# Cross-attention and routed FFN on one core: a ring of eight gathered units, x2 in its own column order, w1 loaded through a permuted view

## The chip, the core and the metric

The kernel runs on one core of a Trainium2 chip. The metric is device time in microseconds, start to end of one execution. The kernel before was run three times unprofiled: 381.10, 386.09 and 389.21 us, median 386.09 us.

## What is computed

The input x is 8 batches of 100 tokens with 512 columns; ctx is 8 batches of 722 rows of 512 columns. Everything is fp32.

```python
def _L0_xattn_ref(x, w1, v1, w2):          # w1 = v1 = w2 = ctx
    x1 = jnp.einsum('eth,efh->etf', x, w1)
    x2 = jnp.einsum('eth,efh->etf', x, v1)
    h = jax.nn.gelu(x1, approximate=True) * x2
    return jnp.einsum('etf,efh->eth', h, w2)
...
def _L0_ffn_ref(h, router_w, w1, b1, w2, b2):
    logits = x @ router_w                   # 16 experts
    assign = jnp.argmax(logits, axis=-1)
    w = jax.nn.sigmoid(jnp.take_along_axis(logits, assign[:, None], axis=1)[:, 0])
    hh = jnp.einsum('nd,edf->nef', x, w1) + b1      # 512 -> 1024
    hh = jax.nn.gelu(hh, approximate=False)
    all_out = jnp.einsum('nef,efd->ned', hh, w2) + b2   # 1024 -> 512
    out = jnp.take_along_axis(all_out, assign[:, None, None], axis=1)[:, 0, :]
    out = out * w[:, None]
...
x = x + _L0_xattn_ref(_layernorm(x, axis=-1), ctx_1024, ctx_1024, ctx_1024)
x = x + _L0_ffn_ref(_layernorm(x, axis=-1), ...)
```

So each of the 800 tokens goes to one of 16 experts, and an expert's weights are 512x1024 (w1) and 1024x512 (w2).

## The kernel before

Work falls into three parts.

**Attention, one batch after another** (NB = 8). TensorE multiplies the layer-normed batch with ctx (`hidden`), ScalarE and VectorE make the gated hidden rows, TensorE multiplies back (`attention`). VectorE adds x (`add_x2`), giving x2, in one of two buffers `xw` of 100 x 4 x 132: four pieces of 128 columns with four more numbers each (a zero, mean, inverse deviation, gate). GpSimd writes a batch's `xw` to the DRAM table `rows` (`put_rows`). Before the change a piece holds columns in a permuted order (`"p (k g r) -> p g k r"`), so that a 32x32 block transpose later gives rows of x in the order in which w1 lies.

**Units.** Tokens are sorted by expert into units of U = 32 tokens. A unit is gathered from `rows` into one slot of the ring `grow` (128 partitions = 4 pieces x 32 tokens) by an indirect DMA of GpSimd (`take`), with indices from the table `lin`. The first four units belong to experts 0 to 3 and are planned from the first six batches alone (`tab_e`, gathered at L887). The table `lin` of all other units (28 here) is made after the last batch: counts on TensorE, `plan_ends`, `token_weights`, `tokens`, `plan_units` on VectorE, `all_slots` on TensorE, `unit_table` on VectorE.

**A unit's work.** VectorE: `fetch` (normalise the gathered rows, and a copy `rb` of them), `turn_tokens` (block transpose to `xT`), `hidden` (transpose and bias, two halves), `residual` and `finish` (scale, add, write to `y`). TensorE: `first_layer` (two halves), `residual` (four matmuls with the identity, which bring x2's rows back to column order), `second_layer`. ScalarE: Gelu. GpSimd, in program order in `step`: copy an index column, wait until the gather of unit i+3 has landed (`landed`), wait for `finish` of its unit, scatter the result to `out` (`put_out`, which then waits for the scatter before it and frees a `y` buffer, of which there are two), and gather unit i+4 (`take`). The order on each engine is the program's order; semaphores tie them. VectorE cannot write `y` (L721) before GpSimd has freed a buffer (`s_yfree`, L838).

**Weights.** SyncE issues every load. There are five slots of w1 and w2 (4 MB of fp32 per expert). Experts 0 to 3 go to `W_early`: one piece (a quarter of an expert, 1 MB) per batch among the ctx loads, eight pieces behind them; expert 4 goes to `area` when ctx has left it. Expert e from 5 on is loaded when expert e-5 has done its last unit: w1 after its first layer (`s_h`), w2 after its second (`s_y`). A piece is one transfer of 128 partitions x 8 KB.

Of the kernel before, what the change touches and what calls it, by code (L numbers as in the profile page):

```python
# [14 lines left out]
P = 128  # L15
# [13 lines left out]
EARLY = 4  # L29
NT = TOK // U - 1  # L30
# [43 lines left out]
def build(nc, x, ctx_main, ctx_rest, ctxT_a, ctxT_b, router, w1, b1, w2, b2, consts, out):  # L74
# [5 lines left out]
    with ExitStack() as stack:  # L80
# [19 lines left out]
        grow = sb("grow", [P, EARLY, ROW])  # L100
        res = sb("res", [P, P])
        unit = sb("unit", [P, 4 * KF * U])
        tb, rb, xT, rT = (sb(n, [P, P]) for n in ("tb", "rb", "xT", "rT"))
        tab_e, lin = sb("tab_e", [P, EARLY], U32), sb("lin", [P, NU], U32)
        idx, at = ([sb(f"{n}{i}", [P, 1], U32) for i in range(2)] for n in ("idx", "at"))
# [5 lines left out]
        zt, gate = sb("zt", [T, 1]), sb("gate", [T, 1])  # L111
# [13 lines left out]
        y = unit[:, 6 * KH * U:8 * KH * U]  # L125
        tok_e = unit[0:T, 0:EB * P].rearrange("p (b q) -> p b q", b=EB)
        tok_all = area[0:T, 2 * WL:2 * WL + NB * P].rearrange("p (b q) -> p b q", b=NB)
# [27 lines left out]
        p_hh, p_r = (p_h[:, 0:P], p_two[:, 0:P]), p_xb[:, 320:320 + P]  # L155
# [5 lines left out]
        s_b2q, s_r = sem("s_b2q"), sem("s_r")  # L161
        s_w = [sems(f"s_w{i}_", 4) for i in range(SLOTS)]
        s_row, s_er = sems("s_row", 2), sems("s_er", EARLY)
        s_g, s_done = sems("s_g", Q), sems("s_done", 2)
# [47 lines left out]
        def _(sp):  # L212
# [21 lines left out]
            def load_w(e, piece):  # L234
                w, src = (W1, w1) if piece < 2 else (W2, w2)
                n = (KD, KF)[piece // 2] // 2
# [14 lines left out]
            for k in range(KD):  # L251
                sp.dma_start(rw[U * k:U * k + U], router.rearrange("(g r) k e -> k r g e", g=Q)[k]).then_inc(s_con, 16)
# [48 lines left out]
        def _(pe):  # L301
# [58 lines left out]
            def all_slots():  # L360
                pe.wait_ge(s_tok, 1)
# [9 lines left out]
            def first_layer(v, e, half):  # L371

                slot, landed = e % SLOTS, 16 * (e // SLOTS) + 16
# [20 lines left out]
            def second_layer(v, e):  # L394

                slot, landed = e % SLOTS, 16 * (e // SLOTS) + 16
                pe.wait_ge(s_yo, v)
                for c in range(KF):
# [7 lines left out]
                last.then_inc(s_y, 1)  # L406
# [3 lines left out]
            for b in range(NB):  # L410
# [5 lines left out]
                hidden(b, 0)  # L416
                if b > 0:
                    transpose_x2(b - 1)
# [5 lines left out]
                else:  # L424
                    pe.wait_ge(s_con, 16 + 16 * KD)
# [8 lines left out]
                if b == FIX + 2:  # L434
                    early_slots()
# [15 lines left out]
            residual(1)  # L451
            logits(NB - 1)
            second_layer(1, 0)
            ranks(NB - 1)
            first_layer(2, 1, 0)
            counts(NB + 1)
            first_layer(2, 1, 1)
            residual(2)
# [3 lines left out]
            residual(3)  # L462
# [3 lines left out]
            residual(4)  # L466
            all_slots()
            second_layer(4, 3)

            def unit_of(e, i):  # L470
                v = pe.snap(i + (EARLY + 1))
                first_layer(v, e, 0)
                first_layer(v, e, 1)
                residual(v)
                second_layer(v, e)
# [5 lines left out]
        def _(act):  # L481
# [21 lines left out]

            copy_rows(xnT, p_t, s_xnps, s_xnT, 0)
# [9 lines left out]

            copy_rows(x2T, p_t, s_x2ps, s_x2T, NB - 1)
# [16 lines left out]
        def _(dve):  # L532
# [137 lines left out]
            def tokens():  # L670
                dve.wait_ge(s_rest, NB)
                nc.vector.tensor_tensor(tok_all, t_row.unsqueeze(1).to_broadcast([T, NB, P]),
                                        rest_all[:, :].unsqueeze(2).to_broadcast([T, NB, P]), ALU.is_equal
                                        ).then_inc(s_tok, 1)

            def unit_table():
                dve.wait_ge(s_linps, 1)
                nc.vector.tensor_scalar(lin[:, :], p_lin, far_col, None, ALU.add).then_inc(s_lin, 1)
# [4 lines left out]
            def row_of(j):  # L683
                at0 = of(j % Q) * ROW
# [23 lines left out]
            def residual(j, v, e):  # L708

                dve.wait_ge(s_r, v)  # L710
                nc.vector.transpose(rT[:, :], rb[:, :])
                nc.vector.scalar_tensor_tensor(out=res[:, :], in0=b2s[:, e, :], scalar=row_of(j)(P + 3, 1), in1=p_r,
                                               op0=ALU.mult, op1=ALU.add).then_inc(s_res, 1)

            def finish(j, v):
# [4 lines left out]
                to = of(j % 2) * P  # L720
# [4 lines left out]
            dve.sem_inc(s_y, 1)  # L725
            nc.vector.memset(p_xb[U * 2:P, 2 * T:3 * T], 0.0).then_inc(s_zero, 1)
            nc.vector.memset(xw[:, :, :, P:P + 1], 0.0)
            nc.vector.memset(first_area[3 * U:P, 0:XR * D + D], 0.0).then_inc(s_zero, 1)
# [6 lines left out]
            dve.wait_ge(s_con, 16 + 16 * KD)  # L735
            for b in range(NB):
# [3 lines left out]
                if b + 1 < NB:  # L740
                    x_stats(b + 1)
                multiply(b, 0)
# [11 lines left out]
                if b == FIX + 2:  # L754
                    early_table()
# [4 lines left out]
            nc.vector.transpose(rT[:, :], rb[:, :]).then_inc(s_res, 1)  # L760
# [8 lines left out]
            residual(0, 1, 0)  # L769
            route(NB - 1)  # L770
            place_rows(NB - 1)
            write_gate(NB - 1)

# [6 lines left out]
            residual(1, 2, 1)  # L780
            plan_ends()
            token_weights()
            tokens()
# [7 lines left out]
            residual(2, 3, 2)  # L791
            plan_units()
# [4 lines left out]
            unit_table()  # L797
# [3 lines left out]
            residual(3, 4, 3)  # L801

            def unit_of(e, i):
# [7 lines left out]
                residual(i + EARLY, v, e)  # L811
# [5 lines left out]
        def _(pool):  # L817
# [13 lines left out]
            def put_out(j, r, index):  # L831

                nc.gpsimd.indirect_dma_start(out_q, bass.IndirectOffsetOnAxis(ap=index, axis=0),  # L833
                                             y[:, P * (r % 2):P * (r % 2) + P], None,
# [5 lines left out]
            def take(i, r):  # L840

                nc.gpsimd.tensor_copy(idx[r % 2][:, :], lin[:, bass.ds(i, 1)]).then_inc(s_idx, 1)  # L842
                pool.wait_ge(s_idx, number(i + 1))
                pool.sem_inc(s_apart_p, 1)  # L844
                nc.gpsimd.indirect_dma_start(grow[:, r, :], None, rows_q,  # L845
                                             bass.IndirectOffsetOnAxis(ap=idx[r % 2][:, :], axis=0),
                                             bounds_check=bound_piece, oob_is_err=False).then_inc(s_g[r], 16)

            def landed(i, r):
                pool.wait_ge(s_g[r], number(4 * i + (16 - 4 * r)))  # L850
                pool.sem_inc(s_rows, 1)  # L851

            def step(i, r):

                nc.gpsimd.tensor_copy(at[r % 2][:, :], lin[:, bass.ds(i, 1)]).then_inc(s_at, 1)  # L855
                landed(i + (Q - 1), (r - 1) % Q)
# [3 lines left out]
                put_out(i + EARLY, r, at[r % 2][:, :])  # L860
                take(i + EARLY, r)

            def early_step(j):
                pool.wait_ge(s_yo, j + 2)
                landed(j - 1, (j - 1) % Q)
# [90 lines left out]
```

## Time and profile before

| | |
|---|---|
| three runs, median | 386.09 us (381.10 to 389.21) |
| the profiled execution | 381.66 us, span 379.6 us, mean granted TensorE clock 0.887 |
| TensorE matmuls busy | 267.8 us, 71% |
| VectorE / ScalarE / GpSimd busy | 137.6 / 39.8 / 103.3 us |
| moved by DMA | 99.46 MB |

The span is the time from the first to the last instruction. The page of the profile cuts it into 40 slices of 9.49 us. "Busy" is instruction time; an engine that waits is not busy. The idle time before an instruction is put down to what released it; GpSimd's "POOLq L838" is its sequencer at line 838. "issue" is waiting that the profile cannot put down to anything. The DMA share is the mean busy share of the core's 16 DMA engines.

### The profile page before, as it was taken

To read this page: it belongs to the slowest core of one execution; us is meant where nothing else is said; L and a number is where in the kernel's file an instruction comes from. 1 tells how busy PE (TensorE), PEld (TensorE's weight loads), DVE (VectorE), ACT (ScalarE), POOL (GpSimd) and SP (SyncE) were. 2 spreads that over 40 slices of the span, in tenths; PEclk is the share of its full clock that TensorE was granted. 3 is DMA by queue.
4 is the path that set the end of the run, shared out by engine and by line. 5 is a ranking of instruction groups with operands and counts; after the bars stand their busy time and mean duration, and the time that the engine had idled before them with its cause. 6 is when DMAs were issued, how large, how long until landed. Compare 5 with 4: busy or idle time off the path is not lost.

```text
span 379.6 us, 12189 instructions
## 1 busy us (share of the span) xinstructions
PE 267.8 (71%) x5032; PEld 228.2 (60%) x5032; DVE 137.6 (36%) x534; ACT 39.8 (10%) x107; POOL 103.3 (27%) x157
## 2 busy tenths in 40 slices
PE   0999989999997956855649456767575667577610
PEld 0868856876693856745548355667474667467510
DVE  3016434644443751532233333222233143525410
ACT  1201111111110200010000000000000001101000
POOL 1002102211114122422234323322232134435451
PEclk9999999999999979896798987688779669989975
DMA  7989999999999992099940999999908940000000
GB/s 267 329 279 299 270 330 342 377 362 347 377 386 412 416 403 82 16 360 416 416 183 11 355 414 418 413 364 377 404 13 321 417 194 16 22 17 23 20 7 6
DMA packets 19704, 99.46 MB, mean 262 GB/s; under 512 B 4072, under 2 KB 4528, under 8 KB 11348
## 3 DMA queue, kind: packets, MB, share of 16 engines
q1 hardware_dynamic: 16852, 93.91, 65.8%
q0 software_dynamic: 2816, 5.03, 4.0%
q8 instruction: 27, 0.44, 0.5%
q14 instruction: 9, 0.07, 0.1%
HBM read 96.33 MB, written 3.82 MB: 264 GB/s over the span
## 4 chain that ended last, share of the span: by engine, by line
DMA 33%; issue 14%; POOL 8%; POOLq 2%
DMA grow<-rows,idx 33%; POOL out L833 6%; POOL idx L842 2%; POOLq L842 0%; POOLq L837 0%; POOL grow L845 0%; POOLq L908 0%; POOLq L858 0%; POOLq L855 0%; POOLq L850 0%; POOLq L844 0%; POOLq L838 0%; POOLq L859 0%; POOLq L851 0%; POOLq L857 0%
## 5 line engine op out<-in xcount | busy, mean ns | idle before, releaser
L403 PE MATMUL bank<-W_early,unit 128*32 128x128 f32 x1600 | 63.9, 326 | 55.6 <-issue 55.5
L403 PEld LDWEIGHTS bank<-W_early,unit 128*32 128x32 f32 x1600 | 56.2, 132 | 61.0 <-issue 60.9
L381 PE MATMUL bank<-W_early,xT 128*32 128x128 f32 x1600 | 58.6, 305 | 11.6 <-DVE xT L696 7.8
L721 DVE SCALAR_TENSOR_TENSOR unit<-bank,grow,res 128x128 f32 (+1 forms) x32 | 11.2, 350 | 140.4 <-POOLq L838 129.5
L381 PEld LDWEIGHTS bank<-W_early,xT 128*32 128x32 f32 x1600 | 52.7, 125 | 15.3 <-DVE xT L696 8.9
L833 POOL DMA_INDIRECT out<-unit,at x28 | 29.1, 1040 | 116.5 <-issue 116.5
L316 PE MATMUL bank<-xnT,area 128*128 128x100 f32 (+1 forms) x384 | 51.7, 290 | 0.6 <-ACT xnT L484 0.6
L316 PEld LDWEIGHTS bank<-xnT,area 128*128 128x128 f32 (+1 forms) x384 | 48.7, 202 | 4.4 <-issue 3.5
L328 PE MATMUL bank<-area,hidT 128*100 128x512 f32 (+1 forms) x96 | 44.7, 604 | 1.8 <-DMA area<-in_ctx_rest 1.6
L501 ACT ACTIVATE unit<-unit 128x128 f32<-128x128 f32 x64 | 19.7, 310 | 215.8 <-DVE unit L703 215.7
L845 POOL DMA_INDIRECT grow<-rows,idx x32 | 35.3, 1102 | 25.6 <-POOL idx L842 24.9
L403 PE MATMUL bank<-area,unit 128*32 128x128 f32 x448 | 18.4, 333 | 15.3 <-issue 15.3
L328 PEld LDWEIGHTS bank<-area,hidT 128*100 128x100 f32 (+1 forms) x96 | 15.2, 171 | 20.3 <-issue 17.7
L403 PEld LDWEIGHTS bank<-area,unit 128*32 128x32 f32 x448 | 16.5, 136 | 16.9 <-issue 16.9
L820 POOL TENSOR_TENSOR xw<-ve_t,con 100x4 f32<-100x4 f32 x8 | 8.5, 1069 | 54.9 <-DVE ve_t L564 54.9
L701 DVE STREAM_TRANSPOSE unit<-bank 128x128 f32<-128x128 f32 x64 | 19.8, 310 | 1.6 <-PE bank L381 1.5
L703 DVE TENSOR_TENSOR unit<-unit,b1s 128x128 f32<-128x128 f32 x64 | 18.9, 295 | 2.2
L553 DVE TENSOR_TENSOR xw<-first_area,bank 100x512 f32<-100x512 f32 x8 | 5.5, 683 | 33.5 <-PE bank L328 33.5
L691 DVE TENSOR_SCALAR tb<-grow 128x128 f32 (+1 forms) x33 | 12.3, 372 | 13.1 <-DMA grow<-rows,tab_e 6.9
L381 PE MATMUL bank<-area,xT 128*32 128x128 f32 x448 | 14.7, 285 | 0.7 <-issue 0.7
L381 PEld LDWEIGHTS bank<-area,xT 128*32 128x32 f32 x448 | 13.5, 117 | 1.2 <-issue 1.1
L390 PE MATMUL bank<-con,rT 128*32 128x128 f32 x256 | 13.6, 277 | 0.0
(89 smaller groups left out, 201.1 us busy)
## 6 DMA issues: line engine op xcount, KB each, us to landing
W_early<-in_w SPq DMA_DIRECT2D x52, 1024.0 KB, 11.8
area<-in_w SPq DMA_DIRECT2D x12, 1024.0 KB, 10.9
area<-in_ctxT_a SPq DMA_DIRECT2D x8, 768.0 KB, 10.6
area<-in_ctx_main SPq DMA_DIRECT2D x8, 768.0 KB
area<-in_ctxT_b SPq DMA_DIRECT2D x8, 676.0 KB, 11.0
area<-in_ctx_main SPq DMA_DIRECT2D x8, 512.0 KB
rows<-xw POOLq DMA_DIRECT2D x8, 206.2 KB, 7.3
first_area<-in_x SPq DMA_DIRECT2D x8, 192.0 KB
```

The source lines that it names most:

```text
L316: last = nc.tensor.matmul(bank_c[0:CW[c], at0:at0 + T], ctxT_part(n)[:, k, P * (c % 3):P * (c % 3) + CW[c]], xnT[:, k, :], start=(k == 0), ...
L328: last = nc.tensor.matmul(p_att[0:T, :], hidT[0:CW[c], c, :], ctx_part(n)[0:CW[c], c % 3, :], start=(c == 0), stop=(c == SC - 1))
L381: last = nc.tensor.matmul(p_hh[half][U * q:U * q + U, :], xT[:, U * k:U * k + U], w[:, q, KH * half:KH * half + KH], start=(k == 0), stop= ...
L390: last = nc.tensor.matmul(p_r[U * q:U * q + U, :], rT[:, U * q:U * q + U], ident, start=True, stop=True, tile_position=(0, U * q))
L403: last = nc.tensor.matmul(p_y[U * q:U * q + U, 0:P], hT[:, c, :], W2[slot][:, c, P * q:P * q + P], start=(c == 0), stop=(c == KF - 1), til ...
L501: nc.scalar.activation(hT[:, KH * half:KH * half + KH, :], hb[half].rearrange("p (c t) -> p c t", c=KH), ACT.Gelu).then_inc(s_act[half], 1)
L691: nc.vector.tensor_scalar(tb[:, :], row(0, P), row(P + 1, 1), row(P + 2, 1), ALU.subtract, ALU.mult)
L701: nc.vector.transpose(hb0[half], p_hh[half]).then_inc(s_hc[half], 1)
L703: nc.vector.tensor_tensor(hb[half].rearrange("p (n t) -> p n t", n=KH), hb0[half].rearrange("p (n t) -> p n t", n=KH), b1s[:, e, :].rearra ...
L721: nc.vector.scalar_tensor_tensor(out=y[:, bass.ds(to, P)], in0=p_y[:, 0:P], scalar=row_of(j)(P + 3, 1), in1=res[:, :], op0=ALU.mult, op1=A ...
L833: nc.gpsimd.indirect_dma_start(out_q, bass.IndirectOffsetOnAxis(ap=index, axis=0), y[:, P * (r % 2):P * (r % 2) + P], None, bounds_check=b ...
L845: nc.gpsimd.indirect_dma_start(grow[:, r, :], None, rows_q, bass.IndirectOffsetOnAxis(ap=idx[r % 2][:, :], axis=0), bounds_check=bound_pie ...
```

## The change

The change has these parts:

- **Columns.** `add_x2` keeps x2's columns in their own order, in plain 128-column pieces. The block transpose then yields rows of x in another order (element 128q + 32g + r on partition 32q + r of slice g), and w1 must lie the same way: `load_w1` fills one slice g at a time from a permuted view of w1. Before, a half of w1 was one transfer, each partition taking one run of 8 KB; now it is two transfers, each partition taking one run of 4 KB, and the source view is led by q, a dimension of 4. The router table lies plainly too: one load where there were four.
- **Residual.** The four identity matmuls of each unit, the copy `rb` and the transpose `rT` go; `residual` reads the gathered rows directly.
- **Ring.** `grow` has 8 slots instead of 4, `y` has 4 buffers instead of 2. A `step` takes unit i+8 and then waits for the gather of unit i+5, which was issued three steps earlier.
- **Boundary.** The table `lin` is made one unit earlier (`all_slots` before the second layer of unit 3), `tokens` is made in two parts, the early gathers are issued ahead of batch 6's rows, and a few instructions are moved. GpSimd gathers four units in a row when `lin` is there.
- A one-element Gelu on ScalarE ahead of the units.

```diff
-                sp.dma_start(w[e % SLOTS][:, n * h:n * h + n], src[e][:, n * h:n * h + n]
-                             ).then_inc(s_w[e % SLOTS][piece], 16)
+                if piece < 2:
+                    load_w1(e, h)
+                else:
+                    sp.dma_start(W2[e % SLOTS][:, KH * h:KH * h + KH], w2[e][:, KH * h:KH * h + KH]
+                                 ).then_inc(s_w[e % SLOTS][piece], 16)
+
+            def load_w1(e, h):
+                src = w1[e].rearrange("(g r) q f -> q r g f", g=Q)
+                for g in range(2 * h, 2 * h + 2):
+                    sp.dma_start(W1[e % SLOTS][:, g, :], src[:, :, g, :]).then_inc(s_w[e % SLOTS][h], 16)
...
-            for k in range(KD):
-                sp.dma_start(rw[U * k:U * k + U], router.rearrange("(g r) k e -> k r g e", g=Q)[k]).then_inc(s_con, 16)
+            sp.dma_start(rw, router).then_inc(s_con, 16)
...
-                slot, landed = e % SLOTS, 16 * (e // SLOTS) + 16
+                slot, landed = e % SLOTS, 32 * (e // SLOTS) + 32
...
-            def residual(v):
-
-                pe.wait_ge(s_res, v)
-                for q in range(Q):
-                    last = nc.tensor.matmul(p_r[U * q:U * q + U, :], rT[:, U * q:U * q + U], ident,
-                                            start=True, stop=True, tile_position=(0, U * q))
-                last.then_inc(s_r, 1)
...
             first_layer(3, 2, 0)
             first_layer(3, 2, 1)
-            residual(3)
+            all_slots()
             second_layer(3, 2)
             first_layer(4, 3, 0)
             first_layer(4, 3, 1)
-            residual(4)
-            all_slots()
             second_layer(4, 3)
...
-                nc.vector.tensor_tensor(xw[:, b % 2, :, 0:P].rearrange("p g (k r) -> p g k r", k=KD),
-                                        xin[0:T, b % XR, :].rearrange("p (k g r) -> p g k r", k=KD, g=Q),
-                                        p_att[0:T, :].rearrange("p (k g r) -> p g k r", k=KD, g=Q), ALU.add
+                nc.vector.tensor_tensor(xw[:, b % 2, :, 0:P], xin[0:T, b % XR, :].rearrange("p (j c) -> p j c", j=Q),
+                                        p_att[0:T, :].rearrange("p (j c) -> p j c", j=Q), ALU.add
                                         ).then_inc(s_x2, 1)
...
-                nc.vector.tensor_scalar(tb[:, :], row(0, P), row(P + 1, 1), row(P + 2, 1), ALU.subtract, ALU.mult)
-                nc.vector.tensor_copy(rb[:, :], row(0, P)).then_inc(signal, 1)
+                nc.vector.tensor_scalar(tb[:, :], row(0, P), row(P + 1, 1), row(P + 2, 1), ALU.subtract, ALU.mult
+                                        ).then_inc(signal, 1)
...
-                nc.vector.transpose(rT[:, :], rb[:, :])
-                nc.vector.scalar_tensor_tensor(out=res[:, :], in0=b2s[:, e, :], scalar=row_of(j)(P + 3, 1), in1=p_r,
+                nc.vector.scalar_tensor_tensor(out=res[:, :], in0=b2s[:, e, :], scalar=row(P + 3, 1), in1=row(0, P),
                                                op0=ALU.mult, op1=ALU.add).then_inc(s_res, 1)
...
             def take(i, r):
 
-                nc.gpsimd.tensor_copy(idx[r % 2][:, :], lin[:, bass.ds(i, 1)]).then_inc(s_idx, 1)
+                to = (r + EARLY) % RING
+                nc.gpsimd.tensor_copy(idx[r % Q][:, :], lin[:, bass.ds(i, 1)]).then_inc(s_idx, 1)
...
             def step(i, r):
 
                 nc.gpsimd.tensor_copy(at[r % 2][:, :], lin[:, bass.ds(i, 1)]).then_inc(s_at, 1)
-                landed(i + (Q - 1), (r - 1) % Q)
                 pool.wait_ge(s_at, pool.snap(i + 1))
                 pool.wait_ge(s_yo, pool.snap(i + (EARLY + 2)))
                 pool.sem_inc(s_apart_p, 1)
-                put_out(i + EARLY, r, at[r % 2][:, :])
-                take(i + EARLY, r)
...
+                put_out(i + EARLY, r % Q, at[r % 2][:, :])
+                take(i + RING, r)
+                landed(i + (RING - 3), (r + RING - 3) % RING)
```

**SyncE, where attention's loads end and the experts' loads go on.** Before (names: destination <- source, shape of the destination as the instruction carries it; the semaphores that it waits for in brackets):

```order
L238 DMA W_early<-in_w 128x2048 x9
L238 DMA area<-in_w 128x2048 [waits s_xps1]
L238 DMA area<-in_w 128x2048
L238 DMA area<-in_w 128x2048 [waits s_att]
L238 DMA area<-in_w 128x2048
L199 TENSOR_LOAD ends [waits s_ends]
```

and with the change, in the same place:

```order
L241 DMA W_early<-in_w 128x2048
L247 DMA W_early<-in_w 128x1x1024 x4
L241 DMA W_early<-in_w 128x2048 x2
L247 DMA W_early<-in_w 128x1x1024 x4
L241 DMA W_early<-in_w 128x2048 x2
L247 DMA area<-in_w 128x1x1024 [waits s_xps1]
L247 DMA area<-in_w 128x1x1024 x3
L241 DMA area<-in_w 128x2048 [waits s_att]
L241 DMA area<-in_w 128x2048
L201 TENSOR_LOAD ends [waits s_ends]
```

The order of the pieces is the same; each w1 piece is two transfers of 4 KB runs, carried with three dimensions instead of two. One other transfer is carried in three dimensions in both kernels, `b_q<-in_b`, also with a source led by a dimension of 4.

**GpSimd, one step of the loop over units.** Before:

```order
L855 COPY at1<-lin 128x1
L850 REGISTER_ALU
L858 REGISTER_ALU [waits s_g2,s_at]
L833 DMA out<-unit,at1 3200x128 [waits s_yo]
L837 ISA
L842 ISA [waits s_done0]
L842 COPY idx1<-lin 128x1
L845 DMA grow<-rows,idx1 128x132 [waits s_idx]
```

and with the change:

```order
L860 COPY at0<-lin 128x1
L861 REGISTER_ALU
L862 REGISTER_ALU [waits s_at]
L837 DMA out<-first_area,at0 3200x128 [waits s_yo]
L841 ISA
L847 ISA [waits s_done1]
L847 COPY idx0<-lin 128x1
L848 REGISTER_ALU
L850 DMA grow<-rows,idx0 128x132 [waits s_idx]
L855 ISA
L860 ISA [waits s_g5]
```

The wait for a gather (`s_g`) has moved from ahead of the scatter to the end of the step, and it is for a gather issued three steps before, where it was for the one issued just before.

## Rows read from the trace of the kernel before

**Rows 1.** The page: DMA in 40 slices (tenths, then GB/s), and its queues.
```profile
DMA  7989999999999992099940999999908940000000
GB/s 267 329 279 299 270 330 342 377 362 347 377 386 412 416 403 82 16 360 416 416 183 11 355 414 418 413 364 377 404 13 321 417 194 16 22 17 23 20 7 6
...
q1 hardware_dynamic: 16852, 93.91, 65.8%
q0 software_dynamic: 2816, 5.03, 4.0%
q8 instruction: 27, 0.44, 0.5%
```
**Rows 2.** The page: the chain that ended last, by engine.
```profile
DMA 33%; issue 14%; POOL 8%; POOLq 2%
```
**Rows 3.** Waits over the span: total us, times, longest.
```profile
DVE unit L721 <- POOLq L838: 129.5, 26, 7.7
```
**Rows 4.** Timeline, one GpSimd step while weights load: start, duration, engine, line.
```profile
179.79 1.14 POOL L845 DMA_INDIRECT grow<-rows,idx  x1 [0.80 <-POOL idx L842]
...
187.77 1.05 POOL L833 DMA_INDIRECT out<-unit,at  x1 [6.64 <-issue]
188.11 0.35 DVE L721 SCALAR_TENSOR_TENSOR unit<-bank,grow,res 128x128 f32 x1 [7.44 <-POOLq L838]
...
189.81 1.14 POOL L845 DMA_INDIRECT grow<-rows,idx  x1 [0.80 <-POOL idx L842]
```
**Rows 5.** Timeline, GpSimd's instructions of one step near the end.
```profile
341.57 1.04 POOL L833 DMA_INDIRECT out<-unit,at  x1 [2.38 <-issue]
...
342.62 0.20 POOL L842 COPY idx<-lin 128x1 uint32 x1
...
343.61 1.03 POOL L845 DMA_INDIRECT grow<-rows,idx  x1 [0.80 <-POOL idx L842]
```
**Rows 6.** Timeline, TensorE: a second layer at half clock, then one unit at full clock.
```profile
179.91 3.64 PE L403 MATMUL bank<-W_early,unit 128*32 128x128 f32 x64 [4.35 <-issue]
...
341.21 2.13 PE L381 MATMUL bank<-area,xT 128*32 128x128 f32 x64
...
343.13 0.43 PE L390 MATMUL bank<-con,rT 128*32 128x128 f32 x8
...
343.76 1.95 PE L403 MATMUL bank<-area,unit 128*32 128x128 f32 x64 [0.20 <-issue]
```
**Rows 7.** Stretches: us, busy by engine, granted clock, DMA share, GB/s.
```profile
60.00:110.00 50.00, 49.50 (x324) 36.05 (x324) 23.64 (x94) 8.12 (x21) 8.25 (x11) 1.00 1.03 360
...
164.00:168.00 4.00, 1.94 (x72) 1.67 (x63) 0.00 (x0) 0.00 (x0) 0.18 (x1) 1.00 1.01 418
...
292.00:296.00 4.00, 0.75 (x16) 0.78 (x20) 2.51 (x10) 0.62 (x2) 2.12 (x3) 0.72 1.02 428
```
**Rows 8.** DMA issues: count, KB each, median us to landing.
```profile
W_early<-in_w SPq DMA_DIRECT2D x52, 1024.0 KB, 11.8
area<-in_w SPq DMA_DIRECT2D x12, 1024.0 KB, 10.9
...
b_q<-in_b SPq DMA_DIRECT2D x1, 32.0 KB
```
**Rows 9.** SyncE's queue in order of time: start, duration.
```profile
9.80 0.78 SPq L253 DMA_DIRECT2D b_q<-in_b  x1
...
161.01 52.03 SPq L238 DMA_DIRECT2D W_early<-in_w  x16
```
**Rows 10.** The DMA packets of the stretch 14.3 to 14.5 us.
```profile
DMA packets 27, 0.06 MB, mean 309 GB/s; under 512 B 0, under 2 KB 19, under 8 KB 27
```
**Rows 11.** Timeline's end (last second layer, last scatter), and the span.
```profile
360.54 1.95 PE L403 MATMUL bank<-W_early,unit 128*32 128x128 f32 x64 [0.85 <-issue]
...
368.86 1.03 POOL L833 DMA_INDIRECT out<-unit,at  x1 [1.92 <-issue]
...
core 0: 379.6 us, clock 0.887
```

More of the change, by code:

```diff
@@ L29 @@
 EARLY = 4
+RING = 8
 NT = TOK // U - 1
@@ L99, in build @@
         x2T = sb("x2T", [P, KD, T])
-        grow = sb("grow", [P, EARLY, ROW])
+        grow = sb("grow", [P, RING, ROW])
         res = sb("res", [P, P])
[L102 to L105, printed above, removed]
+        unit = sb("unit", [P, 3 * KF * U])
+        tb, xT = sb("tb", [P, P]), sb("xT", [P, P])
+        tab_e, lin = sb("tab_e", [P, EARLY], U32), sb("lin", [P, NU + RING], U32)
+        idx = [sb(f"idx{i}", [P, 1], U32) for i in range(Q)]
+        at = [sb(f"at{i}", [P, 1], U32) for i in range(2)]
         ends = sb("ends", [P, E], I32)
@@ L110, in build @@
         top, cand, who = sb("top", [T, 1]), sb("cand", [T, E]), sb("who", [T, 1])
-        zt, gate = sb("zt", [T, 1]), sb("gate", [T, 1])
+        zt, gate, blank = (sb(n, [T, 1]) for n in ("zt", "gate", "blank"))
         hot_all, rank_tmp, rank = sb("hot_all", [T, NB, E]), sb("rank_tmp", [T, E]), sb("rank", [T, 1])
@@ L124, in build @@
         hT = unit[:, 4 * KH * U:6 * KH * U].rearrange("p (c t) -> p c t", c=KF)
-        y = unit[:, 6 * KH * U:8 * KH * U]
         tok_e = unit[0:T, 0:EB * P].rearrange("p (b q) -> p b q", b=EB)
-        tok_all = area[0:T, 2 * WL:2 * WL + NB * P].rearrange("p (b q) -> p b q", b=NB)
+        y = first_area[:, D:D + Q * P]
+        tok_all = first_area[0:T, XR * D - NB * P + D:XR * D + D].rearrange("p (b q) -> p b q", b=NB)
         over = first_area[:, 0:E * (NT + 1)].rearrange("p (e n) -> p e n", e=E)
@@ L384, in first_layer, with second_half @@
                 last.then_inc(s_h[half], 1)
-            def residual(v):
-                pe.wait_ge(s_res, v)
-                for q in range(Q):
-                    last = nc.tensor.matmul(p_r[U * q:U * q + U, :], rT[:, U * q:U * q + U], ident,
-                                            start=True, stop=True, tile_position=(0, U * q))
-                last.then_inc(s_r, 1)
             def second_layer(v, e):
+                second_half(v, e, 0)
+                second_half(v, e, 1)
+            def second_half(v, e, half):
                 slot, landed = e % SLOTS, 16 * (e // SLOTS) + 16
-                pe.wait_ge(s_yo, v)
-                for c in range(KF):
+                if half == 0:
+                    pe.wait_ge(s_yo, v)
+                for c in range(KH * half, KH * half + KH):
                     if c % KH == 0:
@@ L405, in second_layer @@
                                                 start=(c == 0), stop=(c == KF - 1), tile_position=(0, U * q))
-                last.then_inc(s_y, 1)
+                if half == 1:
+                    last.then_inc(s_y, 1)
             pe.wait_ge(s_con0, 16)
@@ L513, in _ @@
                     copy_rows(xnT, p_t, s_xnps, s_xnT, b + 1)
+            nc.scalar.activation(blank[:, :], blank[:, :], ACT.Gelu)
             copy_rows(x2T, p_t, s_x2ps, s_x2T, NB - 1)
@@ L677, in unit_table @@
                 dve.wait_ge(s_linps, 1)
-                nc.vector.tensor_scalar(lin[:, :], p_lin, far_col, None, ALU.add).then_inc(s_lin, 1)
+                nc.vector.tensor_scalar(lin[:, 0:NU], p_lin, far_col, None, ALU.add).then_inc(s_lin, 1)
             def of(x):
@@ L896, in _, with rest @@
             put_out(1, 1, tab_e[:, 1:2])
+            rows_landed(pool, NB - 1)
             pool.wait_ge(s_lin, 1)
-            take(0, 0)
-            take(1, 1)
-            landed(0, 0)
-            early_step(2)
-            early_step(3)
+            for i in range(Q):
+                take(i, i)
+            for i in range(2):
+                landed(i, i)
+                take(Q + i, Q + i)
+            for j in range(2, EARLY):
+                pool.wait_ge(s_yo, j + 2)
+                put_out(j, j, tab_e[:, j:j + 1])
+                landed(j, j)
+                take(Q + j, Q + j)
+            landed(Q, Q)
             pool.wait_ge(s_ends, 1)
             total = pool.value_load(ends[0:1, E - 1:E], min_val=E, max_val=MOST)
-            left = pool.snap(total % Q)
-            whole = pool.snap(total // Q * Q)
-            with pool.Fori(0, whole, Q) as i:
-                for r in range(Q):
-                    step(i + r, r)
-            with pool.If(left > 0):
-                step(whole + 0, 0)
-                with pool.If(left > 1):
-                    step(whole + 1, 1)
-                    with pool.If(left > 2):
-                        step(whole + 2, 2)
+            left = pool.snap(total % RING)
+            whole = pool.snap(total // RING * RING)
+            def rest(r):
+                with pool.If(left > r):
+                    step(whole + r, r)
+                    if r + 2 < RING:
+                        rest(r + 1)
+            with pool.Fori(0, whole, RING) as i:
+                for r in range(RING):
+                    step(i + r, r)
+            rest(0)
             odd = pool.snap(total % 2)
@@ L919, in _ @@
             pool.wait_ge(s_done[1], pool.snap(total // 2 * 16 + 8 * EARLY))
-            for r in range(Q):
-                ahead = pool.snap(total + (EARLY + Q - 1 - r))
-                pool.wait_ge(s_g[r], pool.snap(ahead // Q * 16))
+            for r in range(RING):
+                ahead = pool.snap(total + (2 * RING - 1 - r))
+                pool.wait_ge(s_g[r], pool.snap(ahead // RING * 16))
             pool.sem_inc(s_apart_p, 1)
```

88 lines of the change are left out of this document (41 added, 47 removed).

## The prediction

> **What bounds the kernel now.** I read the page's slices and queues first. The DMA engines are busy at 0.7 to 1.0 in nearly every slice up to slice 15, and again in most slices from 17 to 32, with holes at slices 16, 21 and 29 and nothing behind slice 33 [rows 1]. Then the chain of waits: GpSimd's indirect DMAs hold it, 33% of the span in DMA and 14% in "issue" [rows 2], and VectorE's `finish` waited 129.5 us in 26 goes for GpSimd to free a `y` buffer [rows 3]. Then one step: gather issued at 179.79, next scatter at 187.77, finish at 188.11, next gather at 189.81. A step takes 10.0 us, and the wait ahead of the scatter is for the gather just issued [rows 4]. So behind attention the kernel runs on a loop of GpSimd and one gather's latency. TensorE needs about 4.3 us for a unit at full clock, and a layer goes from 1.95 to 3.64 us at half clock [rows 6]. It isn't the bound there.
>
> Under that loop lies a second bound, and the argument turns on it: weights. The 64 pieces of 1 MB are 67.1 MB [rows 8]. A stretch with nothing but weights in flight moved 418 GB/s at share 1.01, so 414 GB/s for fully busy engines, 25.9 GB/s for each of 16 [rows 7]. An expert (4.19 MB) takes 10.1 us. In attention both resources are full: TensorE 49.5 us of 50, DMA share 1.03 at 360 GB/s [rows 7].
>
> **The change, part by part.**
>
> *Ring of eight, four y buffers.* The gather's latency leaves the step. What stays is scatter 1.04, index copy 0.20, 0.80 to the gather, gather 1.03 [rows 5], and on the other side another index copy of 0.20 with 0.80 behind it: 4.1 us a step, where it was 10.0 under load. For 28 units this is worth up to 28 x 5.9 = 165 us if nothing else took over. Something does: the weights.
>
> *Residual.* Eight TensorE instructions of 0.43 us a unit [rows 6] and two copies on VectorE go. A unit becomes about 4.2 us on TensorE. Both lie beside the wait for weights. I cost this at nothing. If the cover were gone it would be 28 x 0.4 = 11 us.
>
> *Boundary.* The table `lin` comes one unit earlier, about 6 to 8 us (one unit with its second layer). It matters only if the experts' loads wait for it, which begin at 161.01 now [rows 9].
>
> *Router in one load, early gathers moved, blank Gelu.* Each is 1 to 3 us at most, under attention, which is bound by DMA and TensorE. Nothing.
>
> *w1's loads.* Here is the term that decides. Before, a half of w1 is carried as 128 rows on both sides. Now each transfer has a destination of 128x1x1024 and a source view led by a dimension of 4 (32 rows of 4 KB under each). The mechanism I expect: the work of a transfer is dealt to the DMA engines along the outermost dimension, so that a source led by 4 goes to 4 engines with 32 runs each, and always to the same 4. The trace has one transfer of that form, `b_q` (32 KB in runs of 512 B, issued at 9.80 [rows 8, 9]). Its packets should be those of 512 B to 2 KB in 14.3 to 14.5 us: 19 in 0.2 us while DMA is otherwise full [rows 10]. Its 64 packets dealt to 16 engines would be 4 on each. That is thin: the views don't name a packet's engine.
>
> The Trainium skill states the mechanism (DMA: Bandwidth & Descriptors, "Why a DMA increments its semaphore by 16 and not by 1"): the number of engines is the largest up to 16 that divides the size of the slowest dimension of both sides, and the lowest-numbered engines are used. By it w1's transfers run on 4 engines. No row here shows it outright. Its specifications give an engine about 27 GiB/s; by that the w1 term below would be 289 us, and the sum some 35 us lower.
>
> Now the sum for those four engines. Each DMA engine was busy 65.8 + 4.0 + 0.5 = 70.3% of 379.6 us = 266.9 us [rows 1, 11]. The w1 part was 33.55 MB / 414 GB/s = 81.0 us, leaving 185.9 us (ctx, x, w2, rows, gathers, scatters), which the four engines still carry. On four engines w1 takes 33.55 MB / (4 x 25.9 GB/s) = 323.9 us. Together 509.8 us. An expert costs these engines 20.2 us for w1 and 5.1 us for w2, 25.3 us.
>
> Do they run dry? In attention four halves of w1 (iterations 0, 1, 4, 5) each add 10.1 - 2.5 = 7.6 us to the queue, so attention ends some 30 us later, but ctx loads of a batch and a half are always queued behind. Afterwards experts 2 to 4 make 76 us of queue. In that time TensorE does units 1 to 4 and expert 0's remaining units, and the load of expert 5 is asked for before expert 4's has landed. From then on an expert's two units take 9 us at full clock and some 16 us at half, below 25.3, and four loads are queued. So no gap. About 2 us pass before the first packet. SyncE issues 32 transfers more, at 0.4 to 0.8 us each, spread over the span and behind full queues: nothing.
>
> Behind the last weights: the second layer of expert 15's first unit, 1.95; its second unit, 2.13 + 0.6 + 1.95 = 4.7; finish and the way to the scatter, 1; and from the last scatter to the end as now, 379.6 - 368.9 = 10.7 [rows 6, 11]. That is 18.4 us. Now 17.1 us pass from the last second layer's end at 362.5 [rows 11].
>
> Sum: 2 + 510 + 18 = 530 us of span. The profiled execution was 381.66 us for a span of 379.6, and the median of the runs is 4.4 us above it, 1%. I stay at **530 us**: the 186 us contain packets that were slow because all 16 engines were full, which pulls down as much as these pull up.
>
> *Bounds.* From below: w1 at the best rate, 428 GB/s at share 1.02, 26.2 GB/s an engine: 320 us; all other traffic, (93.9 + 5.0 - 33.5) MB [rows 1] / 16 at 25.9 GB/s: 158 us; 20 around them: 498. From above: w1's 4 KB runs at the mixed rate of attention, 360 / 1.03 / 16 = 21.8 GB/s: 385 us, with 186 and 20: 591. I take the weights' rate, as 12 of 16 engines will be half idle and the transfer is long runs of weights. A gain from w1's part isn't possible: the same bytes move in no fewer packets.
>
> **The rivals.**
>
> *The loads stay spread over 16 engines* (or successive ones land on different engines, which comes to the same with several queued). Then GpSimd's loop is gone and weights bind: loads of experts 5 to 15 begin about 8 us earlier, at 153, and take 11 x 10.1 = 111 us, or 11 x 11.1 = 122 with w1 at 21.8 GB/s. With 18 behind them: 282 to 293. TensorE needs 4.2 us a unit at full clock and 7.7 at half [rows 6]; a quarter of the way between, which I choose, is 5.1: 153 + 28 x 5.1 + 15 = 311. About 300 us, faster by a fifth. For it: no row of before shows a large transfer that is confined. Against it: the instruction's form, and the burst of `b_q`. It decides if an engine's share of a w1 transfer is 8 runs and not 32. This is the case on the other side.
>
> *Spread, and the step isn't shortened*, because another wait of `step` (the scatter before it, 3 us under load) takes the gather's place. A step would still be 1.04 + 3 + 2.0 + 1 = 7 us: 28 x 7 = 196, so 153 + 196 + 15 = 364, and with a step left at 8 about 380, no change. The second scatter wait is for one issued a whole step earlier, so this is weak.
>
> *Confined, at the mixed rate*: 591, above; part of my case's range.
>
> **How the numbers follow.** Confined 0.86 (530, own range 498 to 591), spread 0.11 (300), spread with a long step 0.03 (370, half of it within 2%). Range 498 to 592 holds 0.86 of the confined case's 0.95 or so, 0.82. About 2% is what a measurement of this kernel can tell from no change. Faster 0.12, same 0.02, slower 0.86.
>
> **What the profile after would show.** Confined: DMA share near 0.5 or less in the page's slices from the end of attention on, and about 200 GB/s or below; the mean landing of w1's transfers tens of us; TensorE's first layers waiting for DMA into `W_early` and `area` by some 15 to 20 us an expert; attention ending near 148 us; GpSimd's scatters waiting for finish, not for gathers; `finish` no longer waiting at the `y` buffer. Spread: slices full at 400 GB/s behind attention until about 270. Wrong in size, not kind: attention ending at 119 as before would mean that ctx isn't held up, and a share far from (4 x 1 + 12 x 0.2) / 16 = 0.4 would mean another number of engines.

## The result

The changed kernel took 595.45 us (median of 4 runs, 591.12 to 596.90), the kernel before 383.60 us beside it (median of 4, 379.61 to 389.21). The ratio is 1.564, 95% interval 1.548 to 1.580: slower by more than half. The ratio leaves out the slow runs, those over 1.5% above the fastest of their kernel: 386.09 and 389.21 us of the kernel before, and in experiment 1 below 306.13 and 306.86 us. The profiled execution has a span of 594.8 us, and TensorE's mean granted clock was 0.737.

The page of the changed kernel: busy tenths of TensorE, the clock, DMA, GB/s (slices of 14.87 us here, a fortieth of the span), the packets, the main queue, and the chain that ended last, by engine.

```profile
PE   2948079863897128784121242327222424242620
PEclk9989579967797658997657585559565858585955
DMA  8959959869273736454445454545453535354630
GB/s 286 259 160 220 258 195 329 228 179 277 107 204 120 195 111 175 131 175 138 154 138 156 137 161 138 157 132 167 139 174 120 175 126 170 120 164 127 176 106 4
DMA packets 23241, 99.46 MB, mean 167 GB/s; under 512 B 3512, under 2 KB 3968, under 8 KB 18980
q1 hardware_dynamic: 20260, 93.91, 53.0%
...
DMA 43%; SPq 32%; PE 19%; issue 2%; DVE 1%; ACT 1%; POOL 0%; DVEq 0%; POOLq 0%; ACTq 0%
```

The same 99.46 MB are moved. Before, the slices behind attention were nearly full, most of them at 360 to 418 GB/s, with holes between [rows 1]; now they stand at 0.3 to 0.6 and 106 to 195 GB/s until near the end. GpSimd, which held the chain before with its gathers [rows 2], is gone from it. Its place is taken by DMA and by SyncE, whose queue stands still behind transfers that haven't been taken.

Who waits for whom (total us, times, longest), and GpSimd's step:

```profile
POOL out L837 <- DVE first_area L722: 275.0, 28, 26.2
...
PE bank L388 <- DMA W_early<-in_w: 173.6, 20, 12.2
...
PE bank L335 <- DMA area<-in_ctx_rest: 48.1, 4, 20.0
```
```profile
244.21 1.04 POOL L837 DMA_INDIRECT out<-first_area,at  x1 [0.87 <-DMA out<-first_area,at]
...
246.25 1.03 POOL L850 DMA_INDIRECT grow<-rows,idx  x1 [0.80 <-POOL idx L847]
...
248.42 1.03 POOL L837 DMA_INDIRECT out<-first_area,at  x1 [0.94 <-DVE first_area L722]
```

Where weights are there, a step takes 4.2 us from scatter to scatter, against 10.0 before [rows 4], as forecast (4.1). So the ring does what it says. But TensorE's first layers now wait 173.6 us for weights in `W_early` alone, and GpSimd waits 275 us for `finish`.

SyncE's queue (start, us in which the issues stood, line), and the stretches of one expert:

```profile
233.05 22.95 SPq L247 DMA_DIRECT2D W_early<-in_w  x4
256.11 6.15 SPq L241 DMA_DIRECT2D W_early<-in_w  x2
263.17 17.14 SPq L247 DMA_DIRECT2D W_early<-in_w  x4
...
530.89 21.72 SPq L247 DMA_DIRECT2D W_early<-in_w  x4
```
```profile
233.00:239.00 6.00, 5.05 (x152) 4.10 (x156) 3.31 (x12) 0.93 (x3) 3.00 (x5) 1.00 1.02 236
241.00:246.00 5.00, 3.35 (x116) 2.84 (x111) 2.02 (x8) 0.62 (x2) 2.66 (x5) 1.00 0.31 116
...
304.00:312.00 8.00, 2.41 (x48) 2.17 (x48) 0.61 (x2) 0.31 (x1) 0.00 (x0) 0.50 0.26 99
```

From 233.05 to 530.89 ten experts go by, 29.8 us each, where I had forecast 25.3. In the long stretches of an expert DMA stands at share 0.26 to 0.31 and 99 to 116 GB/s: a quarter of 16 engines and a quarter of the 414 GB/s of the full stretches [rows 7]. In the short ones, where w2 is in flight too, all 16 engines are busy (1.02), and yet only 236 GB/s are moved. That second kind of stretch is what the forecast missed. There the packets tell the two loads apart, as w1 moves in packets of 4 KB and w2 in packets of 8 KB. Of the stretch from 233 to 239 us:

```profile
DMA packets 236, 1.42 MB, mean 236 GB/s; under 512 B 20, under 2 KB 20, under 8 KB 106
```

86 packets of w1 are 0.35 MB, 59 GB/s, and 130 of w2 are 1.07 MB, 178 GB/s. In the long stretches what is left of w2 goes along with w1 at a quarter of the engines (54 of the 149 packets from 304 to 312 us are of 8 KB), 99 to 116 GB/s in all.

### The profile page after: what moved, and what is told of

It reads as the page before. It is cut to its first block, busy times and chain, and to the rows that moved or that the text cites. A ratio compares the mean times of both kernels' runs of the same rounds, so it can differ in the third digit from the quotient of the medians.

```text
span 594.8 us, 11687 instructions
## 1 busy us (share of the span) xinstructions
PE 275.8 (46%) x4776; PEld 213.1 (36%) x4776; DVE 129.9 (22%) x470; ACT 40.1 (7%) x108; POOL 106.5 (18%) x165
## 2 busy tenths in 40 slices
DMA packets 23241, 99.46 MB, mean 167 GB/s; under 512 B 3512, under 2 KB 3968, under 8 KB 18980
## 4 chain that ended last, share of the span: by engine, by line
DMA 43%; SPq 32%; PE 19%; issue 2%; DVE 1%; ACT 1%; POOL 0%; DVEq 0%; POOLq 0%; ACTq 0%
DMA W_early<-in_w 31%; SPq L247 19%; SPq L241 10%; DMA area<-in_ctx_rest 7%; PE bank L407 5%; PE bank L323 4%; PE bank L335 4%; PE bank L388 4%; DMA area<-in_w 4%; SPq L225 1%; SPq L277 1%; SPq L233 1%; DMA first_area<-in_x 0%; SPq L232 0%; DVE unit L703 0%
## 5 line engine op out<-in xcount | busy, mean ns | idle before, releaser
L388 PE MATMUL bank<-W_early,xT 128*32 128x128 f32 x1600 | 71.5, 337 | 178.5 <-DMA W_early<-in_w 173.6
L388 PEld LDWEIGHTS bank<-W_early,xT 128*32 128x32 f32 x1600 | 56.0, 135 | 190.6 <-DMA W_early<-in_w 113.7
L837 POOL DMA_INDIRECT out<-first_area,at x28 | 29.1, 1039 | 254.0 <-DVE first_area L722 249.5
L335 PE MATMUL bank<-area,hidT 128*100 128x512 f32 (+1 forms) x96 | 52.1, 687 | 48.1 <-DMA area<-in_ctx_rest 48.1
L407 PEld LDWEIGHTS bank<-W_early,unit 128*32 128x32 f32 x1600 | 49.4, 122 | 35.1 <-issue 32.4
L388 PE MATMUL bank<-area,xT 128*32 128x128 f32 x448 | 18.0, 315 | 38.6 <-DMA area<-in_w 37.8
L722 DVE SCALAR_TENSOR_TENSOR first_area<-bank,grow,res 128x128 f32 (+1 forms) x32 | 11.2, 351 | 82.5 <-PE bank L407 82.5
L388 PEld LDWEIGHTS bank<-area,xT 128*32 128x32 f32 x448 | 14.3, 126 | 41.3 <-DMA area<-in_w 23.7
L407 PE MATMUL bank<-area,unit 128*32 128x128 f32 x448 | 14.8, 279 | 5.8 <-DMA area<-in_w 3.0
L407 PEld LDWEIGHTS bank<-area,unit 128*32 128x32 f32 x448 | 12.2, 112 | 8.8 <-issue 8.2
L847 POOL COPY idx<-lin 128x1 uint32 (+1 forms) x36 | 7.2, 200 | 18.1 <-DMA out<-first_area,at 11.1
```

The lines of the kernel that those rows point to most:

```text
L335: last = nc.tensor.matmul(p_att[0:T, :], hidT[0:CW[c], c, :], ctx_part(n)[0:CW[c], c % 3, :], start=(c == 0), stop=(c == SC - 1))
L388: last = nc.tensor.matmul(p_hh[half][U * q:U * q + U, :], xT[:, U * k:U * k + U], w[:, q, KH * half:KH * half + KH], start=(k == 0), stop= ...
L407: last = nc.tensor.matmul(p_y[U * q:U * q + U, 0:P], hT[:, c, :], W2[slot][:, c, P * q:P * q + P], start=(c == 0), stop=(c == KF - 1), til ...
```

## The experiments

**1. w1 laid in the permuted order ahead of the launch.** One transfer of 128 rows x 8 KB for each half again; all else as changed.

```diff
-                src = w1[e].rearrange("(g r) q f -> q r g f", g=Q)
-                for g in range(2 * h, 2 * h + 2):
-                    sp.dma_start(W1[e % SLOTS][:, g, :], src[:, :, g, :]).then_inc(s_w[e % SLOTS][h], 16)
+                sp.dma_start(W1[e % SLOTS][:, 2 * h:2 * h + 2], w1[e][:, 2 * h:2 * h + 2]
+                             ).then_inc(s_w[e % SLOTS][h], 16)
...
-        "w1": laid(L0_ffn_w1, (E, KD, P, F), (0, 2, 1, 3)),
+        "w1": laid(L0_ffn_w1, (E, Q, Q, U, F), (0, 1, 3, 2, 4)).reshape(E, P, KD, F),
```

> The changed kernel with w1 laid in the permuted order ahead of the launch, so that a half of w1 is again one transfer of 128 rows of 8 KB. All else as changed. Theory A (w1's transfers, led by a dimension of 4, ran on four DMA engines, and their queue set the time): 282 to 316 us, DMA slices near 400 GB/s behind attention. Rival B (something else of the change, say the ring or the boundary, costs the time): above 500 us.

Measured: 304.56 us (median of 4, 301.50 to 306.86; 302.24 by the two that count in the ratio) beside 381.17 us for the kernel before (median of 7, 378.88 to 383.35): 0.79 of it, and 291 us less than the changed kernel. Its page:

```profile
DMA  7999999999999999996299999999999999970000
GB/s 231 349 354 350 344 268 340 362 364 308 395 325 369 385 382 418 423 418 272 51 377 414 407 418 415 415 409 415 414 415 417 417 412 414 412 293 18 12 16 0
```

It holds all that the change does but the form of w1's transfers, and it beats both kernels. So the form costs the time and rival B falls; that it costs it by the number of engines, theory A, is for experiments 3 to 6. The size of my "spread" rival (about 300 us) was right.

**2. The old kernel with nothing but the new load.**

```diff
-                sp.dma_start(w[e % SLOTS][:, n * h:n * h + n], src[e][:, n * h:n * h + n]
+                src = w1[e].rearrange("(g r) q f -> q r g f", g=Q)
+                for g in range(2 * h, 2 * h + 2):
+                    sp.dma_start(W1[e % SLOTS][:, g, :], src[:, :, g, :]).then_inc(s_w[e % SLOTS][h], 16)
```

> The kernel before with nothing changed but the w1 load, which is the changed kernel's (two transfers a half through the permuted view). The rows of w1 so lie in an order that doesn't fit x's, so the experts' results are other numbers; the work is the same. Theory A: 585 to 605 us, as the changed kernel, since the four engines' queue hides the long GpSimd step. Rival B: 380 to 400 us.

Measured: 599.12 us in one run (the kernel before at 381.17). The load alone, put in the old kernel, costs all of it, and the ring, the boundary and the residual's removal bring nothing while it is there: 599 with the old ones, 595 with the new ones.

**3. 4 KB runs, 32 partitions, or the form?** Three variants of the load, the rest as changed. By q from the permuted view (4 transfers of 32 partitions x 2 runs of 4 KB a half):

```diff
+                for q in range(Q):
+                    sp.dma_start(W1[e % SLOTS][U * q:U * q + U, 2 * h:2 * h + 2, :], src[q][:, 2 * h:2 * h + 2, :]
```

> The changed kernel with a half of w1 loaded by four transfers, one for each q, of 32 partitions x 2 runs of 4 KB. The runs are 4 KB and the rows come from the same addresses, but the leading dimension is 32 on both sides. Theory A: within 15 us of the kernel with w1 in host order. Rival C (runs of 4 KB, 16 KB apart, are slow in themselves): more than 60 us above it.

It took 424.53 us, 120 us above experiment 1, with all DMA engines busy and 226 GB/s from 250 to 350 us. That is not theory A's time, and it is within what rival C wants. Two things were mixed in it, so I split them. First, experiment 1's kernel with 128 rows x 4 KB:

```diff
-                sp.dma_start(W1[e % SLOTS][:, 2 * h:2 * h + 2], w1[e][:, 2 * h:2 * h + 2]
+                for g in range(2 * h, 2 * h + 2):
+                    sp.dma_start(W1[e % SLOTS][:, g, :], w1[e][:, g, :]).then_inc(s_w[e % SLOTS][h], 16)
```

> The kernel with w1 in host order, but a half of w1 in two transfers of 128 rows x 4 KB. It splits what was mixed in the transfers by q (424.5 us): runs of 4 KB, and 32 partitions at a time. Theory P (what is slow is that few partitions are written at a time): 300 to 312 us. Rival C (runs of 4 KB are slow): above 350 us.

303.86 us. Runs of 4 KB cost nothing with 128 rows: 409 GB/s from 200 to 250 us, where experiment 1 with its 8 KB runs has 415. Second, experiment 1's kernel in 4 transfers of 32 neighbouring partitions x 8 KB:

```diff
-                sp.dma_start(W1[e % SLOTS][:, 2 * h:2 * h + 2], w1[e][:, 2 * h:2 * h + 2]
+                for q in range(Q):
+                    rows_of_q = slice(U * q, U * q + U)
+                    sp.dma_start(W1[e % SLOTS][rows_of_q, 2 * h:2 * h + 2], w1[e][rows_of_q, 2 * h:2 * h + 2]
```

> The kernel with w1 in host order, but a half of w1 in four transfers of 32 partitions x 8 KB. The other half of the same split. Theory P: 410 to 435 us, as by q with 4 KB, all DMA engines busy at 220 to 230 GB/s. Rival C: 300 to 320 us.

395.72 us, somewhat under the range expected, and 256 GB/s at share 1.02. So it is the transfers of 32 rows, whatever the run. By q with 4 KB runs took another 29 us; it also reads other source addresses (the permuted view), and I haven't taken the two apart.

**4. The same, written to every fourth partition.** The source rows of each transfer stay 32 contiguous ones.

```diff
-                    sp.dma_start(W1[e % SLOTS][rows_of_q, 2 * h:2 * h + 2], w1[e][rows_of_q, 2 * h:2 * h + 2]
+                    sp.dma_start(W1[e % SLOTS][q:P:Q, 2 * h:2 * h + 2], w1[e][rows_of_q, 2 * h:2 * h + 2]
```

> As the kernel with four transfers of 32 partitions x 8 KB (395.7 us), and from the same contiguous source rows in each, but written to every fourth partition (q, q+4, ...) where that one wrote 32 neighbours; w1's rows are laid ahead of the launch so that it comes out right. Theory P (too few neighbouring partitions written at a time): 300 to 315 us, DMA near 400 GB/s. Rival F (32 source rows at a time, or many small transfers, are slow): 385 to 405 us.

308.32 us. Number and size of the transfers, run length and source are those of the 395.72 us; only the partitions written to differ. As many are written at a time, 32, but not as neighbours. Stretches 250 to 300 us of the one with neighbours, 200 to 250 us of the strided one (all engines busy in both):

```profile
250.00:300.00 50.00, 27.28 (x655) 22.74 (x650) 11.89 (x40) 3.10 (x10) 12.71 (x21) 0.73 1.02 256
```
```profile
200.00:250.00 50.00, 38.85 (x1110) 33.66 (x1106) 20.57 (x70) 5.58 (x18) 21.79 (x35) 0.92 1.02 414
```

This agrees with the Trainium skill (SBUF — State Buffer, "Door 1: The DMA port swizzle"), which states that DMA bandwidth hangs on how many of the 16 ports the partitions reach, and that 32 neighbouring partitions reach only 8 of them. The trace shows the rates, not the ports.

**5. Led by 4 with runs of 8 KB.** w1 in host order, in four groups of 33 rows of which the last is unused, so that the two outer dimensions of the source can't be joined.

```diff
+                sp.dma_start(W1[e % SLOTS][:, 2 * h:2 * h + 2, :].rearrange("p g f -> p (g f)"),
+                             w1[e][:, 0:U, 2 * h:2 * h + 2, :].rearrange("q r g f -> q r (g f)")
```

> The changed kernel with w1 laid in the permuted order ahead of the launch, in four groups of 33 rows (the last unused), so that a half of w1 is one transfer of 4 x 32 rows of 8 KB, still led by 4. It asks why an expert took 29.8 us and not the 25.3 that I forecast. Theory D (a transfer led by 4 and a spread one in flight together slow each other, whatever the run): 580 to 600 us, and stretches with both in flight near 230 GB/s. Rival E (the 4 KB runs slow the others down): 520 to 540 us.

597.69 us, as the changed kernel with its 4 KB runs. Theory D's time, and its rate: from 351 to 357 us, with both kinds of load issued, all engines are busy (share 1.02) at 238 GB/s. Rival E falls. What counts is the 4 in front of the source; the 128 partitions of the destination don't undo it.

**6. Led by 8.** The same with eight groups of 17 rows, of which 16 are loaded.

```diff
-                             w1[e][:, 0:U, 2 * h:2 * h + 2, :].rearrange("q r g f -> q r (g f)")
+                             w1[e][:, 0:U // 2, 2 * h:2 * h + 2, :].rearrange("q r g f -> q r (g f)")
```

> The changed kernel with w1 laid in the permuted order in eight groups of 17 rows (the last unused), so that a half of w1 is one transfer of 8 x 16 rows of 8 KB, led by 8 where the other was led by 4. Theory A with my sum on eight engines: 2 + 186 + 162 + 18 = 368 us, with what meeting w2 cost (62 us in all, if it is the same) up to 430. If the width of the leading dimension doesn't matter: 590 to 600 us.

483.86 us. The width matters, as theory A wants, but 8 engines do less than my sum gives them: 368 us by the sum, 430 with the meeting cost of the changed kernel. A stretch in which about half of the engines work, then one in which all do:

```profile
310.00:313.00 3.00, 1.20 (x36) 0.99 (x40) 0.13 (x1) 0.01 (x1) 0.00 (x0) 0.87 0.52 199
```
```profile
320.00:325.00 5.00, 1.08 (x16) 0.66 (x16) 0.00 (x0) 0.00 (x0) 0.00 (x0) 0.50 1.00 228
```

Share 0.52 is 8 of 16 engines. They come near half the full rate at best (199 GB/s of 414), and other such stretches lie at 164 to 188. With all 16 busy it is 228 GB/s again. Why eight engines bring less than their part, and why the total lies above both figures, stays open.

**7. w2 of experts 5 to 15 cut to a sixteenth.**

```diff
-                load_w(e, 2)
-                load_w(e, 3)
+                for h in range(2):
+                    sp.dma_start(W2[e % SLOTS][:, KH * h, 0:P], w2[e][:, KH * h, 0:P]
+                                 ).then_inc(s_w[e % SLOTS][2 + h], 16)
```

> The changed kernel, with the two w2 transfers of experts 5 to 15 cut to 512 B a row, a sixteenth; their second layers work on what else is in the slot, so their outputs are other numbers. It weighs how w2 and w1's narrow transfers meet. My sum gives w2 5.1 us an expert, 4.8 of them gone: 595 - 11 x 4.8 = 542 us. Theory D (in flight together they slow each other, 4.4 us an expert more): 595 - 11 x 9.2 = 494 us.

504.20 us: 91 us less for 11 experts, 8.3 each. w2 weighs more than the 4.8 us of its bytes; theory D's 9.2 is nearer. w1's share of an expert, with almost no w2 beside it, is then close to what I had summed:

```profile
345.12 9.76 SPq L247 DMA_DIRECT2D W_early<-in_w  x4
...
366.14 13.75 SPq L247 DMA_DIRECT2D W_early<-in_w  x4
...
386.05 14.96 SPq L247 DMA_DIRECT2D W_early<-in_w  x4
```

From 260.27 to 451.43 us an expert takes 21.2 us on average (19.2 to 22.1); the sum had 20.2 for w1, and 0.3 for this sixteenth of w2. GpSimd's queue, which the sum held in another term, takes 2.8% of the engines' time here: 0.6 us of an expert, if it is spread evenly.

**8. Never together.** SyncE waits for w1 to land before w2, and for w2 before the next w1, for experts 5 to 15.

```diff
+                for h in range(2):
+                    sp.wait_ge(s_w[e % SLOTS][h], 32 * (e // SLOTS) + 32)
                 load_w(e, 2)
                 load_w(e, 3)
+                for h in range(2):
+                    sp.wait_ge(s_w[e % SLOTS][2 + h], 16 * (e // SLOTS) + 16)
```

> The changed kernel, but SyncE waits until w1 of an expert (5 to 15) has landed before it issues w2, and until w2 has landed before the next expert's w1, so the narrow and the wide transfers are never in flight together there. Theory D (it is their meeting that slows both): w2 alone at 350 to 415 GB/s, w1 alone near 100; an expert takes 20.4 + 5.1 us and two landings of about 2, 29 to 30 us, so the total stays at 585 to 605 us. If w2's transfers are slow in this kernel by themselves: stretches with w2 alone near 240 GB/s and a total of 630 us or more.

628.47 us. The total is above theory D's range, but the stretches decide for it: w1 alone, then w2 alone:

```profile
387.00:405.00 18.00, 1.08 (x16) 0.65 (x16) 0.00 (x0) 0.00 (x0) 2.46 (x4) 0.50 0.26 104
410.00:414.00 4.00, 1.39 (x31) 0.96 (x24) 1.06 (x4) 0.32 (x2) 0.00 (x0) 0.50 0.96 408
```
```profile
384.25 5.14 SPq L247 DMA_DIRECT2D area<-in_w  x4
407.90 0.82 SPq L241 DMA_DIRECT2D area<-in_w  x2
416.50 2.57 SPq L247 DMA_DIRECT2D W_early<-in_w  x4
```

w2 alone runs at 408 GB/s and w1 alone at 104, where in the changed kernel the two together have 236. From w1's issue to w2's is 23.65 us, from there to the next w1 8.60: 20.2 and 5.1 of transfer with some 3.5 us of landing and issue after each. I had put 2 us, hence the total. The parts by themselves cost what the sum said; their meeting is what it left out. Keeping them apart is no remedy, as the waits cost more than the meeting did.

**9. The ring's worth.** Experiment 1's kernel with one wait more in a step, for the gather just issued.

```diff
                 take(i + RING, r)
+                pool.wait_ge(s_g[r], number(2 * (i + RING) + (16 - 2 * r)))
```

> The kernel with w1 in host order (304.6 us) plus one wait in each GpSimd step, for the gather that the step has just issued, as the kernel before waits. It gives the ring's part by itself. If the gather's latency in the step was what bound the kernel before, as I read it: 360 to 385 us. If the ring of eight isn't what gives the gain over the kernel before: 300 to 320 us.

374.61 us. GpSimd's steps:

```profile
200.96 1.03 POOL L836 DMA_INDIRECT out<-first_area,at  x1 [0.87 <-POOL at L859]
...
208.61 0.18 POOL L859 COPY at<-lin 128x1 uint32 x1 [4.59 <-DMA grow<-rows,idx]
209.66 1.05 POOL L836 DMA_INDIRECT out<-first_area,at  x1 [0.87 <-POOL at L859]
...
219.32 1.04 POOL L836 DMA_INDIRECT out<-first_area,at  x1 [0.87 <-POOL at L859]
```

Steps of 8.7 and 9.7 us, as before the change, and 70 of the 77 us between the old kernel's 381.2 and experiment 1's 304.6 are back (the old kernel beside this run took 385.5). The reading of the old bound [rows 4] was right.

## Why the prediction was right in its direction and outside its range

- **What bound the kernel before.** Right: experiment 9 gives 374.6 us for one wait put back.
- **The ring shortens the step to 4.1 us.** Right: 4.2 us where nothing else holds it. **Weights take its place.** Right: 595 with the new ring, 599 with the old.
- **w1's transfers run on as many DMA engines as the source's leading dimension has members.** Right for 4 and 8: share 0.26 with w1 alone, led by 4; 0.52 led by 8; full when led by 32 or 128. Experiments 1, 5 and 6 differ in little else. Here the trace agrees with the rule of the Trainium skill (DMA: Bandwidth & Descriptors, "Why a DMA increments its semaphore by 16 and not by 1") that the prediction cited. That these are the same four engines each time follows from the rate, 104 GB/s with four transfers queued; the views don't name them.
- **w1 on four engines: 20.2 us an expert.** Right: 21.2 in experiment 7, of which about 0.9 are the rest of w2 and GpSimd's queue.
- **The step that failed is the sum "an expert costs these engines 20.2 us for w1 and 5.1 us for w2, 25.3 us".** It lets the narrow and the wide transfers run together at the rates that each has alone. An expert took 29.8 us. In stretches like 233 to 239 us, about 8 to 9 us in each expert, both are in flight, all 16 engines are busy, and 236 GB/s pass instead of 414; w1 gets 59 of them instead of 104. By an estimate from these rates, which takes it that the four engines carry only w1 meanwhile, that costs the four engines 8.5 x (1 - 59 / 104) = 3.7 us an expert. From the other side: GpSimd's queue takes 3.0% of the engines' time from 233 to 531 us, 0.9 us an expert if spread evenly, and the sum held it in its 186 us; 29.8 - 25.3 - 0.9 leaves 3.6 us for the meeting. For the 14 experts from expert 2 on that is 50 us. With 20 us more in attention and 4 less in the tail (both below) it makes 66, and the miss is 594.8 - 530 = 65.
- **The range.** Its upper end came from w1's runs at attention's mixed rate. That was the wrong bound: run length costs nothing in transfers of 128 rows (303.9 us with 4 KB). That this bound, 591, comes within 5 us of the measured time is chance. The loss that was there had no row before the change, since no narrow transfer of size ran there. Such an unknown asked for a wider upper side.
- **Attention ends near 148 us.** It ended at 168, 48 us later than before instead of 30. TensorE waited four times for ctx, 48.1 us in all, 12 for each half of w1 where the sum had 7.6. From 25 to 30 us, with narrow w1 pieces beside wide ctx loads, all engines are busy at 204 GB/s, so the meeting costs there too; how much of the 12 us it makes I haven't taken apart.
- **The tail, 18.4 us.** It was 14: the last weights are there at 580.6, and the last matmuls end at 581.6 of 594.8. Expert 15 has one unit behind its last weights, and the sum had put in a second one, 4.7 us.
- **Residual, boundary, router at nothing.** They are hidden, as 599 against 595 shows. In experiment 1 they aren't separated from the ring beyond the 7 to 11 us that experiment 9's 374.6 lies under the old kernel's 381.2 to 385.5.

Why the meeting halves the rate stays open. That 32 neighbouring partitions written at a time limit the rate is shown (experiment 4), but the wide loads' twelve other engines write partitions all over, and they slow down too. Whether the four engines' writes hold up others on the way or the reads collide wasn't tried.

## What to carry to other kernels

A view that makes a load fit can change on how many DMA engines it runs: look at the outermost dimension of the source of a large transfer too, and not only at the destination's, and put the 128 partitions there, if need be by laying out the tensor ahead. Spread the partitions of one transfer too, as 32 neighbours gave 256 GB/s and every fourth one 414. A DMA share of a clean fraction of one (0.25, 0.5) with a full queue is the sign of the first; a full share at half the rate is a sign of the second or of a narrow load beside a wide one. And a gain on one resource (here some 70 us from the ring) is nothing until the next bound under it has been priced.

## What the runs showed that I had not expected

- A narrow and a wide load together moved 236 GB/s with all 16 engines busy, where the one alone has 104 on four engines and the other 408. Both slow down: w1 to 59, w2 to 178.
- Stretches with about eight engines busy brought 164 to 199 GB/s, not 207.
- Transfers to 32 neighbouring partitions moved 256 GB/s, and the same ones to every fourth partition 414.
- SyncE's issues stood for 23 us where each takes under a microsecond when the queue is empty: 22.95 us for four transfers at 233.05, 0.82 for two at 407.90 in experiment 8.
